# Level weights at distances two and four from overlaid broadcast rows, with one ring of four PSUM banks

## The reference

```
q, k, v = xn Wq', xn Wk', xn Wv'                  (128 channels a head)
G = cumsum(-softplus(xn Wg' + bg))                (one number per token and head)
lam = softplus(xn Wdl' + Lparam)                  (12 levels per token and head)
level(t, s) = 0 if t = s, else floor(log2(t - s)) + 1
A[t, s] = (q_t . k_s) / sqrt(128) * exp(G_t - G_s) * lam[t, level(t, s)]     for s <= t
y = A v ;  out = layernorm(y Wo' + x) ;  x = x + out
```

## Time and profile before

| | us |
|---|---|
| median of 3 runs (1408.34 to 1414.47) | 1411.46 |
| the profiled execution | 1405.15 |
| its span, first to last instruction | 1403.3 |
| PE busy, share of the span | 1299.5, 93% |
| ACT busy | 1104.5, 79% |
| DVE busy | 1082.8, 77% |
| POOL busy | 792.7, 56% |

### The profile page before, as it was taken

How to read it: one execution, slowest core, us unless ns; L and a number is a source line. 1 busy time by engine, 2 the same in 40 slices (tenths; PEclk the granted TensorE clock), 3 DMA queues, 4 the chain that set the end, 5 groups by cost and what they waited for, 6 DMA issues and landing times.

```text
span 1403.3 us, 31442 instructions
## 1 busy us (share of the span) xinstructions
PE 1299.5 (93%) x10278; PEld 1137.4 (81%) x10278; DVE 1082.8 (77%) x2724; ACT 1104.5 (79%) x3270; POOL 792.7 (56%) x956
## 2 busy tenths in 40 slices
PE   4699899999999999999999999999999999989997
PEld 4588788888888788787888888887888878878875
DVE  4767767798868977689777988679886797767776
ACT  3589879888788877897788977888778887778732
POOL 2154457734585455953578444864558545595562
PEclk9899999999999999999999999999999999999998
DMA  5311122112221121111221122211212112211200
GB/s 180 113 45 51 43 70 70 42 43 59 58 72 44 50 73 54 44 50 44 73 73 50 44 58 58 67 44 37 71 46 73 50 44 59 72 45 30 67 9 16
DMA packets 125725, 80.37 MB, mean 57 GB/s; under 512 B 50569, under 2 KB 115323, under 8 KB 125435
## 3 DMA queue, kind: packets, MB, share of 16 engines
q1 hardware_dynamic: 124472, 77.85, 20.2%
q10 hardware_dynamic: 1090, 0.51, 0.2%
HBM read 67.64 MB, written 10.09 MB: 55 GB/s over the span
## 4 chain that ended last, share of the span: by engine, by line
PE 47%; ACT 16%; DVE 12%; POOL 11%; SPq 6%; issue 4%; DMA 3%; ACTq 0%; POOLq 0%; DVEq 0%
PE o_ps L1603 11%; ACT w_all L844 6%; PE s_ps L1523 4%; PE l_ps L1546 4%; PE aux L1523 4%; PE s_ps L1525 4%; PE s_ps L1524 4%; POOL a_lo_all L692 4%; PE aux L1524 3%; PE aux L1525 3%; SPq L456 3%; ACT a_hi L892 3%; DVE a_all L1150 2%; PE aux L1616 2%; SPq L469 2%
## 5 line engine op out<-in xcount | busy, mean ns | idle before, releaser
L692 POOL TENSOR_TENSOR a_lo_all<-a_all,a_hi 128x256 fp32r<-128x256 f32 (+2 forms) x576 | 575.5, 1016 | 526.2 <-ACT a_hi L892 524.4
L844 ACT ACTIVATE w_all<-l_ps,bias 128x128 f32<-128x128 f32 x1589 | 439.3, 388 | 43.8 <-PE l_ps L1546 42.4
L1150 DVE TENSOR_TENSOR a_all<-s_ps,w_all 128x512 f32<-128x512 f32 (+3 forms) x768 | 360.6, 483 | 132.6 <-PE s_ps L1525 87.9
L1603 PE MATMUL o_ps<-a_hi,v_all 128*128 128x256 f32 (+2 forms) x1152 | 396.7, 353 | 1.7 <-POOL a_lo_all L692 1.7
L892 ACT ACTIVATE a_hi<-a_all 128x256 fp32r<-128x256 f32 (+2 forms) x576 | 300.1, 547 | 75.5 <-DVE a_all L1150 73.7
L1523 PE MATMUL s_ps<-q_hi,xt_hi 128*128 128x256 f32 (+2 forms) x576 | 224.8, 390 | 31.1 <-DVE a_all L1150 29.3
L1603 PEld LDWEIGHTS o_ps<-a_hi,v_all 128*128 128x128 f32 x1152 | 218.1, 189 | 23.1 <-POOL a_lo_all L692 1.8
L1525 PE MATMUL s_ps<-q_hi,xt_lo 128*128 128x256 f32 (+2 forms) x576 | 195.1, 339 | 0.0
L1524 PE MATMUL s_ps<-q_lo,xt_hi 128*128 128x256 f32 (+2 forms) x576 | 194.7, 338 | 0.0
L1603 PE MATMUL o_ps<-a_lo_all,v_all 128*128 128x256 f32 (+2 forms) x576 | 194.4, 338 | 0.0
L1523 PEld LDWEIGHTS s_ps<-q_hi,xt_hi 128*128 128x128 f32 x576 | 109.8, 191 | 43.9 <-DVE a_all L1150 22.8
(11 more groups left out here) (259 smaller groups left out, 2617.5 us busy)
## 6 DMA issues: line engine op xcount, KB each, us to landing
far<-ef_scratch SPq DMA_DIRECT2D x64, 320.0 KB, 3.6
rb<-eb_scratch SPq DMA_DIRECT2D x1016, 0.8 KB
farther<-ef_scratch SPq DMA_DIRECT2D x64, 192.0 KB, 3.3
ra<-ea_scratch SPq DMA_DIRECT2D x508, 4.0 KB, 2.1
rc<-ea_scratch SPq DMA_DIRECT2D x508, 4.0 KB, 1.6
mt<-m_scratch SPq DMA_DIRECT2D x62, 128.0 KB, 3.5
nt<-n_scratch SPq DMA_DIRECT2D x62, 128.0 KB, 3.5
tx<-in_L_attn_x SPq DMA_DIRECT2D x9, 512.0 KB, 5.6
```

Source lines behind the costliest of these rows:

```text
L692: pool.tensor_tensor(a_lo[r][:, 0:t1 - t0], a[r][:, 0:t1 - t0], a_hi[r][:, 0:t1 - t0].bitcast(F32), ALU.subtract).then_inc(a_lo_done, 1)
L844: last = act.activation(w[k][:, W_AT[j] + d, :].rearrange("p (f c) -> p f c", f=2), l_tiles[:, :, :, i - i0], ACT.Exp, bias=bias[b % 2][:, ...
L1150: dve.tensor_tensor(a[(n * NG + g) % NA][:, 0:t1 - t0], s_ps[:, g % 2, 0:t1 - t0], w[n % 2][:, at:at + (t1 - t0) // P, :].rearrange("p i n ...
L1603: last = pe.matmul(o, lhs[:, vr, j, :], rhs[r][:, 0:t1 - t0], start=fresh, stop=True, skip_group_check=True)
```

## The change

- Units 2 and 3, `rb`, its masks, its scratch in DRAM and its part of the level logarithms go. `far` goes too.
- Three rows are loaded to all partitions instead, with one buffer each: `row8` and `row9` of 6 tiles, `row10` of 4 (384 + 384 + 256 KB a turn). VectorE overlays them by a predicated copy with a triangular mask: in `row8`, level 9 over level 8 where the key stands before the mark, for d = 2; in `row10`, level 9 over level 10, for d = 4. ScalarE takes 5, 6 and 4 exponentials from rows 9, 8 and 10, at groups 5, 7 and 8 of its own order. VectorE's copies stand at places 17 (`row10`) and 32 (`row8`).
- SP loads the rows for turn n+2 once the last exponential of turn n+1 is done, ahead of the farther row.
- `s_ps` and `l_ps` become one `ring` of four banks. A rule at build time gives each score one bank and each level unit two neighbouring ones, the longest unused, and TensorE waits for their last holders.
- Unit 1 moves from group 3 to group 4, and the tables of places are new.

```diff
-UNITS = [[(0, 0, 8)], [(1, 1, 7)], [(2, 2, 6)], [(4, 4, 4)]]
+UNITS = [[(0, 0, 8)], [(1, 1, 7)]]
...
-U_AT = {0: 0, 3: 1, 5: 2, 8: 3}
-FAR_AT = {8: 0}
-B_AT = {21: 0}
-S_AT = {30: 0}
-C_OUT = {31: 0}
-X_AT = {41: 0}
+U_AT = {0: 0, 4: 1}
+FAR_AT = {5: 0, 7: 1, 8: 2}
+SEL_AT = {17: 1, 32: 0}
+NFAR = 3
+B_AT = {16: 0}
+S_AT = {28: 0}
+C_OUT = {32: 0}
+X_AT = {44: 0}
...
-DVE_MORE = {0: [('t_stat', 2)], 1: [('t_stat', 1)], 3: [('t_stat', 0)], 13: [('stat1', 1), ('t_stat', 3)],
...
-            110: [('t_low', 1)], 126: [('z', 1)], 130: [('x_low', 0)], 133: [('x_low', 1)], 147: [('gate', 0)],
-            150: [('gate', 1)], 165: [('gate', 2)], 181: [('gate', 3)], 185: [('softplus', 0)],
-            186: [('softplus', 1)], 190: [('up', 0)], 195: [('guard', 0)], 203: [('sums', 0)], 206: [('up', 1)],
-            213: [('log', 0)], 218: [('log', 1)], 228: [('up', 2)], 232: [('l_low', 0)], 236: [('decay', 0)],
-            240: [('up', 3)], 242: [('l_low', 1)], 244: [('up', 4)], 259: [('up', 5)], 274: [('up', 6)],
...
+DVE_MORE = {7: [('t_stat', 2), ('t_stat', 1)], 9: [('t_stat', 0), ('t_stat', 3)], 15: [('stat1', 1)], 20: [('o', 1)],
...
+            122: [('z', 1)], 133: [('x_low', 0)], 136: [('x_low', 1)], 144: [('gate', 0)], 153: [('gate', 1)],
+            173: [('softplus', 0)], 182: [('gate', 2)], 184: [('softplus', 1)], 195: [('gate', 3)], 197: [('up', 0)],
+            204: [('guard', 0)], 205: [('sums', 0)], 206: [('log', 0)], 210: [('up', 1)],
+            227: [('log', 1), ('l_low', 0)], 236: [('up', 2)], 238: [('up', 3), ('decay', 0)], 240: [('l_low', 1)],
+            242: [('up', 4)], 252: [('up', 5)], 274: [('up', 6), ('up', 7)], 295: [('up', 8)], 308: [('up', 9)],
...
+NRING = 4
+RING, RING_BEFORE = {}, {}
+_since, _holder = [-NRING + _k for _k in range(NRING)], {}
+def _take(user, count):
+    first = min(range(NRING - count + 1), key=lambda k: (max(_since[k:k + count]), min(_since[k:k + count])))
+    RING[user] = list(range(first, first + count))
+    RING_BEFORE[user] = [_holder[_k] for _k in RING[user] if _k in _holder]
+    for _k in RING[user]:
+        _holder[_k] = user
+        _since[_k] = len(RING)
...
+        row8, row9, row10 = sb("row8", [P, NR]), sb("row9", [P, NR]), sb("row10", [P, NT4])
...
+            def load_rows(eng, n):
+                b, h = divmod(n, H)
+                for level, row in ((8, row8), (9, row9), (10, row10)):
+                    at = NR - row.shape[1]
+                    eng.dma_start(row[:, :], ef_dram[b, h * HIGH + level - LOW, at:].partition_broadcast(P)).then_inc(rows_in, 16)
...
+                def load_next_rows(n):
+                    sp.wait_ge(far_done, NFAR * n)
+                    sp.wait_ge(t["stored"], EL * (n // H + 1))
+                    load_rows(sp, n)
...
+                def row_exps(n, part):
+                    d, row = ((3, row9), (NEAR, row8), (TOP, row10))[part]
+                    if part == 0:
+                        act.wait_ge(rows_in, ROWS_IN * (n + 1))
+                    else:
+                        act.wait_ge(selected[part - 1], n + 1)
...
+                def select_rows(n, part):
+                    dst, src, where = ((row8, row9, after), (row10, row9, until))[part]
+                    dve.wait_ge(rows_in, ROWS_IN * (n + 1))
+                    tiles = dst.shape[1] // P
+                    dve.copy_predicated(dst[:, :].rearrange("p (i n) -> p i n", n=P),
+                                        where[:, None, :].broadcast_to([P, tiles, P]),
+                                        src[:, NR - tiles * P:].rearrange("p (i n) -> p i n", n=P)).then_inc(selected[part], 1)
...
+                def wait_ring(user):
+                    before = RING_BEFORE[user]
+                    weighed = [n * NG + g + 1 for kind, n, g in before if kind == "scores"]
+                    levelled = [n * NU + u + 1 for kind, n, u in before if kind == "unit"]
+                    if weighed:
+                        pe.wait_ge(a_done, max(weighed))
+                    if levelled:
+                        pe.wait_ge(w_done, max(levelled))
```

More of the change, by code:

```diff
@@ L51 @@
 F16 = mybir.dt.float16
+U8 = mybir.dt.uint8
 BF16 = mybir.dt.bfloat16
@@ L77 @@
 _at = 0
-for _name, _n in (("ma0", NTA * P), ("ma1", NTA * P), ("mb2", NTB * P), ("mb4", NTB * P),
-                  ("ident", P), ("tri", P), ("suf", P), ("first", E), ("off", TA)):
+for _name, _n in (("ma0", NTA * P), ("ma1", NTA * P), ("ident", P), ("tri", P), ("suf", P), ("first", E), ("off", TA)):
     CONST[_name] = (_at, _at + _n)
@@ L257 @@
 LAST_CHAIN = 5
+NRING = 4
[8 more added lines that the diff above has]
+        _since[_k] = len(RING)
+_take(("unit", 0, 0), 2)
+for _n in range(NH):
+    for _g in range(NG):
+        _take(("scores", _n, _g), 1)
+        if _g in U_AT and _n + 1 < NH:
+            _take(("unit", _n + 1, U_AT[_g]), 2)
 AUX_AT = {}
@@ L291, in main_stage @@
         rc = [sb(f"rc{k}", [P, TA, NTA, NC], F16) for k in range(2)]
-        rb = [sb(f"rb{k}", [KB, TB, NTB, NC], F16) for k in range(2)]
-        far = [sb(f"far{k}", [P, NF]) for k in range(2)]
-        farther = [sb(f"farther{k}", [P, NF - (FAR[1][0] - FAR0) * P]) for k in range(2)]
+        row8, row9, row10 = sb("row8", [P, NR]), sb("row9", [P, NR]), sb("row10", [P, NT4])
+        after, until = (sb(n, [P, P], U8) for n in ("after", "until"))
+        farther = [sb(f"farther{k}", [P, NQ]) for k in range(2)]
         q_hi = [sb(f"q_hi{k}", [P, T], F32R) for k in range(2)]
@@ L487, in token_dst, with score_bank @@
             return x_key[b % 2][:, i, :] if i < NS else tx[:, i, :]
-        EL_ROWS = ((0, NA_ROWS, TA), (NB_AT, NB_END, TB))
         def l_region(n, u):
-            return l2_ps if n == 0 and u % 2 else l_ps
+            if n == 0 and u:
+                return l2_ps
+            k0, k1 = RING[("unit", n, u)]
+            return ring[:, k0:k1 + 1, :]
+        def score_bank(n, g):
+            return ring[:, RING[("scores", n, g)][0], :]
         def mean_var(dve, b, part, stats, mv, ve, s_st, s_mv, s_ve):
@@ L848, in exps @@
                     last.then_inc(w_done, 1)
-                def far_exps(n):
+                def row_exps(n, part):
                     k = n % 2
                     b, h = divmod(n, H)
-                    act.wait_ge(far_in[k], 16 * (n // 2 + 1))
-                    for j in range(NC - FAR0):
-                        last = act.activation(w[k][:, W_AT[j] + FAR0, :], far[k][:, j * P:(j + 1) * P], ACT.Exp,
-                                              bias=bias[b % 2][:, h, BIAS_AT[FAR0] + j:BIAS_AT[FAR0] + j + 1])
+                    d, row = ((3, row9), (NEAR, row8), (TOP, row10))[part]
[3 more added lines that the diff above has]
+                        act.wait_ge(selected[part - 1], n + 1)
+                    first = NC - row.shape[1] // P
+                    for j in range(NC - d):
+                        at = (j + d - first) * P
+                        last = act.activation(w[k][:, W_AT[j] + d, :], row[:, at:at + P], ACT.Exp,
+                                              bias=bias[b % 2][:, h, BIAS_AT[d] + j:BIAS_AT[d] + j + 1])
                     last.then_inc(far_done, 1)
@@ L1037, in _ @@
                 farther_exps(0)
-                far_exps(0)
+                for part in range(NFAR):
+                    row_exps(0, part)
                 act.wait_ge(s_rows, 1)
@@ L1476, in _ @@
                     first_v(u)
+                dve.wait_ge(preds, 2)
+                for part in range(2):
+                    select_rows(0, part)
                 for u in range(Q_U):
@@ L1491, in _ @@
                             first_query(1, late[:, 1, 0:NQ])
+                        if place in SEL_AT and n + 1 < NH:
+                            select_rows(n + 1, SEL_AT[place])
                         if place in C_OUT:
@@ L1837, in _ @@
                         turn_expert_weights()
-                    if u < 2:
-                        value(0, u + 2)
-                    if u in (2, 3):
-                        scores(0, u - 2)
-                    if u == 3:
-                        for k in range(Q_U):
-                            query(1, k)
+                    value(0, u + 2)
+                for g in range(2):
+                    scores(0, g)
+                for k in range(Q_U):
+                    query(1, k)
                 wait_taken(pe, ("q", 1, 0))
@@ L1866, in _ @@
                     piece(kind, n, i)
-                    keep_busy(s_ps[:, 1, :], idle.get((kind, i), 0))
+                    keep_busy(ring[:, 3, :], idle.get((kind, i), 0))
                 for hh in range(2 * NC):
```

170 lines of the change are left out of this document (66 added, 104 removed), and 10 rows, old and new, of tables (DVE_MORE, PE_MORE).

## The result

The changed kernel takes 1454.72 us (median of 4 runs, 1451.83 to 1456.96), the kernel before 1410.98 in the same session: a ratio of 1.031, 95% interval 1.028 to 1.034. I had forecast 1408, with 1379 to 1436 as the range. It is slower, and the time lies outside the range.

The account below looks back on a forecast made before the run. TensorE bounds the kernel now, VectorE its fourth and fifth turns; after the change both nearly level. -0.5 us a batch over seven (-3.5) and +0.2 at the start took 1411.46 to 1408 us, range 1379 to 1436.

Parts of the forecast that it names:

- the copy's wait for GpSimd: VectorE's two copies each turn: 0.3 us wait each, 0.6 together; bounds nothing and 0.96 us each.
- my own sign of being wrong: Steady batch: expected at 164 to 166 us; below 162 or above 168 would show the forecast wrong.
- TensorE's gain: 16 of 48 level matmuls a turn go: at most 0.58 us a turn, 4.6 a batch, 37 over 63 turns.
- The ring: Four banks in turn for scores and level units: taken as 0, bound 4.1 us a batch either way.
- The copies' ordinary cost: VectorE's two copies, 0.95 and 0.68 us plus waits: 2.25 us a turn, 18.0 a batch; 1.0 to 3.6 a turn.
- The sum: Whole kernel: -3.5 us over seven batches and +0.2 at the start, -3.3 on 1411.46, forecast 1408 us.
- its own range of 1398 to 1418: Whole kernel: range of the forecast case itself, without the rivals, given a chance of 0.38.
- the 83.8 us for the last four turns: Last four turns of a batch, 82.9 us before: taken as 83.8, +0.9.
- Rival 1: Last four turns TensorE's, copies unwaited or in VectorE's idle time: -4.6 us a batch, -32, 1379 us; chance 0.30.
- Rival 2: VectorE bounds the fifth turn, 28.3 us of work against 22.2: +4.1 a batch, +29, 1440 us; chance 0.26.
- Rival 3: Row loads by DMA land late, 7.6 us against 6.5 in the shortest turn: +1.5 a batch, 1418 us; chance 0.06.
- Start: First product: a statistic waiting 1.02 us moves away, two selections (1.63) come in: +0.2 us.

Follow-up runs that it names:

- the best version: Changed kernel with GpSimd's second-turn scalings, shift and additions moved to places 76 to 79 and its seventh-turn base to 309: 1407.24 us, ratio 0.9984.
- early hand-over: Changed kernel where GpSimd waits, before its first scaling in the second turn (not batch 0), for VectorE's row 8 copy: 1417.07 us, ratio 1.0035.
- the moved train: Changed kernel with GpSimd's second-turn scalings, shift and additions moved from places 58 to 78 to places 76 to 79: 1411.52 us, ratio 1.0012.
- the one with four: Kernel before with only the four-bank rule added, for its scores and its four level units a turn: 1457.60 us, ratio 1.035.

## Why the prediction was wrong

**The failed step: the copy's wait for GpSimd.** I wrote "a copy that starts at any moment waits for 0.6 x 0.5 = 0.3 us", with 0.96 us as the bound. Both rest on one operation: VectorE waits at most for the GpSimd operation in progress. That holds for 122 of the 128 copies (none waited more than 0.94 us); in six it was 8.6 us. A steady batch above 168 us was my own sign of being wrong; batch 3 took 174.3. I took the bound from rows of waits that had been short, and never looked at how long GpSimd's stretches without a gap are where the new copies would stand. My own text had GpSimd "busy for 60% of a batch", a mean; in the second turn of the kernel before it ran 24 operations end to end, from 569.0 to 587.8. The delay goes both ways: in the first turn the copy lengthened GpSimd's next low part from 0.73 to 1.52 us. The products, with their scores in PSUM, show no such wait: the longest of the 192 with 512 columns took 0.693 us, before and after the change, against a mean of 0.682. For the six long copies one operation is far too little a bound: they waited for the one in progress and for seven that started after the copy had arrived.

**TensorE's gain: not refuted, and not measured alone.** I had 4.6 us a batch, 37 in all, as the most that fewer matmuls can give. Without the copies the kernel is 49 us faster, but there the ring and the new places count as well, and no run takes them apart. TensorE's batch, which I had at 153 us, is 156.7 in the changed kernel at a granted clock of 0.96 and 154.4 in the best version at 0.99.

**The ring: the second wrong term.** I took 0, bounds of 4.1 us a batch on either side. It is worth 33 us, 4.2 a batch: my bound, and not the 0. I had weighed the waits of the kernel before (29.3 us before the wider scores over the whole run); with the change and without the ring the same waits are 48.3. That the copies are what raised them is likely but not shown: no run leaves out both the copies and the ring.

**The copies' ordinary cost: too large in work, too small in time.** I counted 2.25 us a turn; VectorE's busy time without copies and with them at an early hand-over is 1062.5 and 1167.1 us, 1.63 a turn. In time they cost 54 us, 0.86 a turn, half of that work. I had a steady batch 0.5 us shorter than before; in the hand-over kernel it is 4.1 longer (169.51 us in batch 3 against 165.4), while batch 0, which I had left as it was, is 8.2 shorter (145.7 against 153.9).

**The sum, had there been no long wait.** 1417.1 by the hand-over, 1411.5 by the moved train, against 1408 and its own range of 1398 to 1418. (In the sum itself, the 83.8 us for the last four turns was a choice: it lies above both numbers that I had worked out, 82.4 and 80.6, and no row gives it. They took 85.6 us in the changed kernel, with VectorE busy for 76.1 and not 82.3.) The errors of the ring (33 us too slow) and of the copies had opposite signs, so that is partly luck.

**Rival 1, 1379 us.** It did not come: the copies' ordinary work alone costs 49 to 54 us. Only the kernel without the copies is that fast or faster, at 1362.9.

**Rival 2, the fifth turn, 1440 us.** Place right, size wrong: 24.48 us against 22.2, with VectorE busy for 23.70, so 2.3 instead of 6.1. I had counted 28.3 us of work. Of the 4.6 too many, the copies are 0.4 (0.76 and 1.05 us there, not 2.25) and gate step 3 is 0.7 (2.5 us from first to last, with one wait for GpSimd where the earlier trace rows have two); the rest I did not trace.

**Rival 3, late rows.** Wrong. VectorE waited for the rows 6 times in 64 turns, 4.6 us in all; they land in 4.1 and 4.7 us:

```profile
row<-ef_scratch SPq DMA_DIRECT2D x128, 384.0 KB, 4.1
row<-ef_scratch SPq DMA_DIRECT2D x64, 256.0 KB, 4.7
```

**Start.** The first product starts at 60.70 us instead of 60.31; I had +0.2.

## What to carry to other kernels

Before a VectorE instruction with its operands in SBUF is added (here a predicated copy; no other kind was tried), look at the timeline of GpSimd where it will stand, not at GpSimd's mean load: the price may be the whole stretch in which GpSimd runs end to end (8.6 us here), and everything behind the instruction pays it (7.5 us of idle time on TensorE, 8.1 on ScalarE). In the profile this wait had no idle time (0.0 before the copy's row); compare median and maximum of the instruction's line (1.056 and 9.666 us). The cure is cheap: place it where GpSimd has a gap, or let one GpSimd operation wait for the end of the one before it (0.14 us here), or hand over by a semaphore. Of the three, the first took 43 us off the changed kernel and the third 38; the second was seen in one batch of one kernel, and its worth in time is not measured.

A ring of banks should be judged by the waits that the rest of the change will make, not by those of the kernel before, and by how many users share it: it gave 33 us in the kernel with two units a turn and cost 48 in the one with four. More differs between these two kernels than the number of units, so that number is my reading of the waits, and no run shows it alone.

## What the runs showed of the hardware

- A predicated copy of 768 fp32 columns with a uint8 mask takes 1.05 us, one of 512 takes 0.74 to 0.75, one of 432 0.65.
- Such a copy waited through 5 to 14 GpSimd operations without a gap, and then took 6.1 to 10.5 us. A gap of 0.14 us let it in.
- Beside a one-tensor scaling of 512 columns on GpSimd the copy took 1.36 us, though the scaling in progress had 1.33 us to go when it arrived: the two ran at the same time.
- The granted clock was 0.83 in the second turn of batch 3, in which TensorE stood idle for 7.5 us behind VectorE's copy, 0.95 there with the early hand-over and 1.00 with the train moved. With the early hand-over it was also 0.91 in the third turn, in which TensorE was busy for 20.73 of 20.88 us. What lowers the clock is not shown.
